# Four f32 projections of a decoder layer's chunk loop computed from high and low parts, with the loop's steps reordered on every engine

## The chip, the cores and the metric

The kernel runs on one core of a Trainium2 chip. The metric is the device time of one launch in microseconds (us). It was run three times, and the median is the time quoted.

## The reference

One decoder layer over x of shape (8, 512, 256): gated slot attention, cross-attention to 64 context rows per batch, and a top-2 mixture of eight experts. What matters here, cut:

```python
x = x + attn(layernorm(x))
    q, k = silu(x @ Wq), silu(x @ Wk);  v = x @ Wv
    f = log_sigmoid(x @ Wf) / 8;  s = 1 - exp(f)
    # recurrence over t: hk = hk*exp(f) + k s^T;  p = softmax(q hk);  hv = hv*exp(f) + s v^T;  o = p hv
    return rmsnorm(o) @ Wo
x = x + xattn(layernorm(x), ctx)      # softmax with distance bias; out @ W_o.T
x = x + ffn(layernorm(x))             # router, top 2 of 8, capacity 1280, W2(silu(W1 x) * W3 x)
```

## The kernel before, in words

The 4096 tokens are 32 chunks of 128. The first half of the program, the **chunk loop**, takes one chunk per step and is software-pipelined: each engine has a hand-written list in its own `step(run)`, and `run(lag, work)` does `work` for the chunk that is `lag` steps back. After 32 steps there are `LAGS` more, the **drain**. The second half, the **expert stage**, runs 40 groups of 256 rows and begins when the last routed row has been sent to memory by POOL (`send_rows`, indirect transfers).

The order of everything in the loop is set by these lists and by two kinds of semaphore wait: an operand's (`pe.wait_ge(f_cols_ok, n + 1)`), and a PSUM bank's, where `turns` lists which tiles share each of the eight banks and `bank_left` waits until the tile before has been read.

One chunk goes, in the program's names:

- DVE normalizes (`f_xn`, helper `norm`, L944), PE transposes it (`f_columns`, L1379), ACT copies it to SBUF as `f_xnt` (`evacuate`, L721).
- PE projects (`product`, L1385): `project_vf` for v and the gate (weights 128x512), `project_qk` for q, transposed (128x128), and k (128x256). Every operand is f32, and an f32 matmul runs as two passes: two records each.
- ACT: `f_absolute` (abs, exp, ln of the gate, L785 to L794), `qk_sigmoid` (three passes, L799 to L805), `one_minus`, `gates` (`down`, `decay`, `up`). DVE: `log_gates` (`g_s`, L1022), `queries_keys`, `slot_values` (`s_s`), then the state `hk`, `hv`. POOL adds two chunks' gates (`both_gates`, `g_both`, L603) and does the small powers of each norm.
- PE: `sum_states`, `sum_gates`, transposes, `scores`, `logits`; DVE, ACT and DVE do the softmax, PE transposes it (`p_columns`), ACT copies it (`p_t`), PE does `mix` and `read_out`, and `o_columns` / `project_o` give the block's output `y`, 128x256. The cross-attention follows with `x_scores`, `e_columns`, `values`, `x_outputs` (DVE, `xo_t`), `x_project_o` (`xy`, 128x256) and `residual2`; the router with `top_two` and `places` (DVE) and `send_rows` (POOL).

At the start, the first step also builds the context tables: `context_keys` (PE, and ACT's copies `k_all`, L776), `context_values`, and DVE's `small_tables`, which SP's `key_biases` waits for before it loads further rows of x. During the drain, `behind(c)` splits two of the six pieces of the first expert's weights after each of the drain's first three steps: the high half on ACT (L876), the low half on DVE (L1289, 128x1024 each).

The expert stage already multiplies split operands:

```python
def split_product(dst, pairs):
    return product(dst, [(lhs[i], rhs[k]) for lhs, rhs in pairs for i, k in ((0, 0), (0, 1), (1, 0))])
```

Its tiles are of type F32R, written as `hi = copy(t)` and `lo = t - hi`; each F32R matmul is one record.

## Time and profile before

| | us |
|---|---|
| runs | 1402.39, 1397.52, 1398.87; median 1398.87 |
| profiled execution, its own time | 1398.93 |
| its span, first to last instruction | 1397.2 |
| chunk loop, steady: from the normalization (`f_xn`) of chunk 3 to that of chunk 31 | 74.4 to 626.9, 19.73 a chunk |
| drain: from there to the last transfer that POOL issues | 626.9 to 702.0 |
| first matmul of the expert stage's tiles to the end | 707.4 to 1397.2 |
| busy: PE, DVE, ACT, POOL over the span | 93%, 67%, 46%, 30% |

The profile's busy shares are averages over stages with different limits. In the expert stage PE works almost without a gap; in the chunk loop PE and DVE are both close to full, ACT is a little over half busy. A row of a timeline gives start, duration, engine, line, operation, tiles and count, and in brackets how long the engine had been idle before it and what ended that. An instruction's result is visible a little after its duration ends, and the next independent instruction of the same engine can start before it ends.

### The profile page before, as it was taken

How to read it: one execution, taken by the hardware profiler on the slowest of the kernel's cores; microseconds unless marked ns; L12 is line 12 of the kernel's file. 1: busy time of each engine (PE TensorE's matmuls, PEld its weight loads, DVE VectorE, ACT ScalarE, POOL GpSimd, SP SyncE).
4: the chain of work that ended last, by engine and by line, in shares of the span. 5: the costliest groups of instructions: out<-in, count | busy, mean ns of one | idle time of the engine just before them, and what ended most of it. 6: DMA issues, size and time to landing. Idle time of an engine off the chain costs nothing.

```text
span 1397.2 us, 33423 instructions
## 1 busy us (share of the span) xinstructions
PE 1299.0 (93%) x11085; PEld 1153.5 (83%) x11085; DVE 931.1 (67%) x2770; ACT 640.2 (46%) x1628; POOL 417.4 (30%) x741
## 2 busy tenths in 40 slices
PE   7799999999999999998579999999999999999996
PEld 5577777777777777776369999999999999999996
DVE  5578888888888888887546565565645656565442
ACT  2355555555555555554344344443434435444331
POOL 4114334443444344433302122222221222211112
PEclk9899999999999999997579999999999999999999
DMA  3821210100101010100042242423524334252212
GB/s 96 248 86 34 96 54 25 34 30 30 33 26 34 26 34 25 34 23 24 27 132 31 32 121 32 122 33 48 116 33 113 37 64 94 34 123 32 31 24 24
DMA packets 152459, 80.20 MB, mean 57 GB/s; under 512 B 106210, under 2 KB 145859, under 8 KB 152290
## 3 DMA queue, kind: packets, MB, share of 16 engines
q1 hardware_dynamic: 137698, 59.11, 16.6%
q0 software_dynamic: 14592, 18.91, 7.9%
q8 instruction: 97, 1.59, 0.5%
q14 instruction: 72, 0.59, 0.1%
HBM read 44.04 MB, written 33.96 MB: 56 GB/s over the span
## 4 chain that ended last, share of the span: by engine, by line
PE 80%; DVE 7%; ACT 6%; issue 4%; DMA 1%; POOL 1%; SPq 0%; ACTq 0%; DVEq 0%; POOLq 0%
PE banks L1385 65%; PE banks L1494 4%; PE banks L1379 3%; PE banks L1569 2%; PE banks L1580 2%; PE banks L1489 2%; ACT qk_l L801 1%; ACT qk_e L799 1%; PE banks L1565 1%; DVE r_st L933 1%; DVE hk L1058 1%; DMA xin<-in_x 1%; ACT p_t L721 1%; ACT one_less L811 1%; DVE hv L1059 1%
## 5 line engine op out<-in xcount | busy, mean ns | idle before, releaser
L906 ACT ACTIVATE h_a<-banks 128x256 f32<-128x256 f32 x320 | 122.3, 382 | 348.1 <-PE banks L1385 333.1
L1316 DVE TENSOR_TENSOR h_f<-banks,h_a 128x256 f32<-128x256 f32 x320 | 135.6, 424 | 144.4 <-ACT h_a L906 119.7
L521 POOL TENSOR_TENSOR idle_g<-half 128x1 f32<-128x1 f32 x144 | 32.0, 222 | 533.4 <-DVE y_s L1335 383.0
L1385 PE MATMUL banks<-xe_t_hi,w_even_hi 128*128 128x256 f32 x640 | 180.6, 282 | 3.6 <-issue 2.1
L1385 PE MATMUL banks<-xe_t_hi,w_even_lo 128*128 128x256 f32 x640 | 180.4, 282 | 0.9 <-issue 0.9
L1385 PE MATMUL banks<-xe_t_lo,w_even_hi 128*128 128x256 f32 x640 | 180.4, 282 | 0.0
L1385 PE MATMUL banks<-xe_t_hi,w_odd_hi 128*128 128x256 f32 x640 | 178.2, 279 | 0.0
L1385 PE MATMUL banks<-xe_t_lo,w_odd_hi 128*128 128x256 f32 x640 | 178.2, 278 | 0.0
L1385 PE MATMUL banks<-xe_t_hi,w_odd_lo 128*128 128x256 f32 x640 | 178.2, 278 | 0.0
L895 ACT ACTIVATE h_t_hi<-h_f 128x256 fp32r<-128x256 f32 x320 | 131.7, 412 | 32.6 <-DVE h_f L1316 32.1
L1323 DVE TENSOR_TENSOR h_t_lo<-h_f,h_t_hi 128x256 fp32r<-128x256 f32 x320 | 133.6, 417 | 6.0 <-ACT h_t_hi L895 3.4
L700 POOL DMA_INDIRECT out_dram<-y_s,token x80 | 127.7, 1596 | 26.0 <-issue 19.2
L1385 PEld LDWEIGHTS banks<-xe_t_hi,w_even_hi 128*128 128x128 f32 x640 | 123.5, 193 | 4.2 <-issue 4.2
L1385 PEld LDWEIGHTS banks<-xe_t_hi,w_even_lo 128*128 128x128 f32 x640 | 122.4, 191 | 1.2 <-issue 1.2
L1385 PEld LDWEIGHTS banks<-xe_t_lo,w_even_hi 128*128 128x128 f32 x640 | 122.4, 191 | 0.0
L1385 PEld LDWEIGHTS banks<-xe_t_hi,w_odd_hi 128*128 128x128 f32 x640 | 121.4, 190 | 0.0
L1385 PEld LDWEIGHTS banks<-xe_t_lo,w_odd_hi 128*128 128x128 f32 x640 | 120.1, 188 | 0.0
L1385 PEld LDWEIGHTS banks<-xe_t_hi,w_odd_lo 128*128 128x128 f32 x640 | 120.1, 188 | 0.0
L1385 PE MATMUL banks<-w_in,f_xnt 128*128 128x512 f32 (+1 forms) x256 | 96.7, 500 | 0.5 <-ACT f_xnt L721 0.5
L1333 DVE CAST token<-about 128x1 uint32<-128x1 f32 x78 | 8.4, 149 | 127.0 <-PE banks L1385 127.0
L1385 PE MATMUL banks<-w_odd_hi,h_t_hi 128*128 128x256 f32 x320 | 89.1, 278 | 1.8 <-DVE h_t_lo L1323 1.8
L1385 PE MATMUL banks<-w_even_hi,h_t_hi 128*128 128x256 f32 x320 | 89.0, 278 | 0.0
(244 smaller groups left out, 3399.6 us busy)
## 6 DMA issues: line engine op xcount, KB each, us to landing
raw<-in_w SPq DMA_DIRECT2D x24, 1024.0 KB, 5.0
expert_rows<-empty SPq DMA_DIRECT2D x4, 2580.0 KB, 10.9
x_blocks<-expert_rows SPq DMA_DIRECT2D x312, 32.0 KB
xin<-in_x SPq DMA_DIRECT2D x32, 128.0 KB, 2.2
out_dram<-x SPq DMA_DIRECT2D x32, 128.0 KB, 1.7
out_dram<-y_s,token POOLq DMA_INDIRECT x80, 4.0
mask_i<-in_mask SPq DMA_DIRECT2D x32, 32.0 KB, 1.9
expert_rows<-r_xn,send POOLq DMA_INDIRECT x64, 2.6
```

The lines of the kernel that those rows point to most:

```text
L521: return pool.tensor_tensor(idle_g[:, i:i + 1], half[:, 0:1], half[:, 0:1], ALU.add)
L700: pool.indirect_dma_start(out=out, out_offset=bass.IndirectOffsetOnAxis(ap=token[par][a][:, :], axis=0), in_=y_s[:, par, a, :], in_offset= ...
L895: act.activation(h_t[0][:, par, f, :], h_f[:, f % 2, :], ACT.Copy).then_inc(h_hi_ok, 1)
L906: act.activation(h_a[:, f % 2, :], bank[2 + f % 4][:, 0:GS], ACT.Silu).then_inc(silu_ok, 1)
L1316: dve.tensor_tensor(h_f[:, f % 2, :], bank[2 + f % 4][:, GS:2 * GS], h_a[:, f % 2, :], ALU.mult)\
L1323: dve.tensor_tensor(h_t[1][:, par, f, :], h_f[:, f % 2, :], h_t[0][:, par, f, :], ALU.subtract)\
L1379: last = pe.transpose(dst[0:t.shape[1], i * P:(i + 1) * P], t, ident[:, :])
L1385: last = pe.matmul(dst, lhs, rhs, start=(i == 0), stop=(i == len(pairs) - 1))
L1489: pe.matmul(dst[:, m * P:(m + 1) * P], queries[:, m, :], states[:, m, :], start=True, stop=False)
L1494: last = pe.matmul(dst[:, cols], weights[:, h, :], rows[:, cols], start=False, stop=(h % 2 == 1))
L1569: last = pe.matmul(tile[f"x_scores{i}"][:, k * D:(k + 1) * D], xq_t[rows, k, :], k_bd[rows, k, :, :].rearrange("p h k -> p (h k)"), start= ...
L1580: last = pe.transpose(tile[f"e_cols{k}"][:, j * P:(j + 1) * P], pair, ident[:, :])
```

## The change

Four products of the chunk loop (v and gate, k, the attention's output, the cross-attention's output) take tiles of type F32R in a high and a low part, `hi*hi + hi*lo + lo*hi`, in place of one f32 product. The q projection stays f32. Chunk 0 still projects v, gate and k in f32.

```diff
+            def three(rows, weights, cols):
+                return [(rows[i][:, k, :], weights[j][:, k, cols]) for k in range(KT) for i, j in ((0, 0), (0, 1), (1, 0))]
...
             def project_vf(n, c, b):
-                pe.wait_ge(f_cols_ok, n + 1)
...
+                else:
+                    pe.wait_ge(f_lo_ok, n + 1)
+                    if n == 1:
+                        pe.wait_ge(weights_lo_ok, 1)
+                    pairs = three(f_part, w_in_part, slice(D, 3 * D))
                 bank_left(pe, "vf", n)
-                product(tile["vf"], [(f_xnt[:, k, :], w_in[:, k, 2 * D:4 * D]) for k in range(KT)]).then_inc(vf_mm, 1)
+                product(tile["vf"], pairs).then_inc(vf_mm, 1)
...
             def project_o(n, c, b):
-                pe.wait_ge(o_ok, n + 1)
+                pe.wait_ge(o_lo_ok, n + 1)
...
-                product(tile["y"][:, 0:D], [(o_t[:, k, :], wo_s[:, k, :]) for k in range(2)]).then_inc(y_mm, 1)
+                product(tile["y"][:, 0:D], three(o_part, wo_part, slice(0, D))).then_inc(y_mm, 1)
```

The parts are made by new instructions: ACT writes `f_hi` beside `f_xnt` and `xo_hi`, POOL writes `f_lo` and `xo_lo`, ACT's copy of the attention output becomes `o_hi` and DVE writes `o_lo`.

```diff
             def f_columns(n, c, b):
-                evacuate(n, f_xnt[:, :, :], two(tile["f_cols"][:, 0:D]), f_cols_mm, qk_mm, f_cols_ok)
+                if later(n, 1):
+                    act.wait_ge(qk_mm, n)
+                    act.wait_ge(f_lo_ok, n)
+                act.wait_ge(f_cols_mm, n + 1)
+                act.activation(f_xnt[:, :, :], two(tile["f_cols"][:, 0:D]), ACT.Copy)
+                act.activation(f_part[0][:, :, :], two(tile["f_cols"][:, 0:D]), ACT.Copy).then_inc(f_cols_ok, 1)
+                if not later(n, 1):
+                    act.wait_ge(vf_landed, 32)
+                    act.wait_ge(qk_landed, 32)
+                    act.activation(w_in_part[0][:, :, :], w_in[:, :, 0:3 * D], ACT.Copy).then_inc(weights_hi_ok, 1)
...
+            def f_low(n, c, b):
+                pool.wait_ge(f_cols_ok, n + 1)
+                if later(n, 1):
+                    pool.wait_ge(qk_mm, n)
+                pool.tensor_tensor(f_part[1][:, :, :], f_xnt[:, :, :], f_part[0][:, :, :], ALU.subtract).then_inc(f_lo_ok, 1)
+                if not later(n, 1):
+                    pool.wait_ge(weights_hi_ok, 1)
+                    pool.tensor_tensor(w_in_part[1][:, :, :], w_in[:, :, 0:3 * D], w_in_part[0][:, :, :], ALU.subtract)\
+                        .then_inc(weights_lo_ok, 1)
+            def xo_low(n, c, b):
...
+                pool.wait_ge(xo_hi_ok, n + 1)
+                pool.tensor_tensor(xo_part[1][:, :, :], xo_t[:, :, :], xo_part[0][:, :, :], ALU.subtract).then_inc(xo_lo_ok, 1)
...
+            def xo_high(n, c, b):
...
+                act.wait_ge(xot_ok, n + 1)
+                act.activation(xo_part[0][:, :, :], xo_t[:, :, :], ACT.Copy).then_inc(xo_hi_ok, 1)
...
+            def o_low(n, c, b):
+                dve.wait_ge(o_ok, n + 1)
+                dve.tensor_tensor(o_part[1][:, :, :], two(tile["o_cols"][:, 0:D]), o_part[0][:, :, :], ALU.subtract).then_inc(o_lo_ok, 1)
...
                 for k in range(KT):
                     dve.tensor_scalar(wo_s[:, k, :], wo_raw[:, k, :], gn[:, 0:1], None, ALU.mult).then_inc(small_made, 1)
+                dve.wait_ge(small_made, KT)
+                dve.tensor_copy(wo_part[0][:, :, :], wo_s[:, :, :]).then_inc(small_made, 1)
+                dve.wait_ge(small_made, KT + 1)
+                dve.tensor_tensor(wo_part[1][:, :, :], wo_s[:, :, :], wo_part[0][:, :, :], ALU.subtract).then_inc(small_made, 1)
```

To make room in SBUF, the third weight matrix of the even experts moves behind the chunk loop's tiles, so its two pieces of expert 0 are split in the first expert group and not in the drain:

```diff
             def behind(c):
-                if c < 3:
+                if c < 2:
                     for piece in (2 * c, 2 * c + 1):
                         split_weights(0, 0, piece)
...
+                    if is_last(g, 0) and f in (1, 2):
+                        split_weights(0, 0, 3 + f)
```

The four lists are reordered, and their beginnings moved round (`LAGS` is 6 for that reason; a lag that is one higher at a list's start is the same place in the program as one lower at its end). POOL's new list is `both_gates, r_power, values, x_power, keys, f_power_later, hidden_keys, send_rows, f_low, xo_low, head_power`. PE, from the transposes of `f_xn` (`sum_states` adds k and v to the states; `before` and `all_b` are the router's counts); before:

```order
L1379 MATMUL banks<-ident,f_xn 128x128 x2
...
L1385 MATMUL banks<-w_in,f_xnt 128x512 x2
L1385 MATMUL banks<-f_xnt,w_in 128x128 x4
L1385 MATMUL banks<-w_in,f_xnt 128x256 x2
L1385 MATMUL banks<-both,before 128x8
L1385 MATMUL banks<-both,all_b 128x8
L1385 MATMUL banks<-s_s,k_s 64x64 x4
L1385 MATMUL banks<-v_s,s_s 64x64 x4
L1385 MATMUL banks<-g_s,tri_half 128x256
```

and in the change:

```order
L1446 MATMUL banks<-ident,f_xn 128x128 x2
...
L1452 MATMUL banks<-s_s,k_s 64x64 x4
L1452 MATMUL banks<-v_s,s_s 64x64 x4
L1452 MATMUL banks<-w_in_hi,f_hi 128x512
L1452 MATMUL banks<-w_in_lo,f_hi 128x512
L1452 MATMUL banks<-w_in_hi,f_lo 128x512
...
L1452 MATMUL banks<-f_xnt,w_q 128x128 x4
L1452 MATMUL banks<-w_in_hi,f_hi 128x256
...
L1452 MATMUL banks<-both,before 128x8
```

`sum_states` now stands between `read_out` (left out in both) and `project_vf`. DVE, from the end of `places` to the router's statistics (`zk`, `zv` are `end_states`, `x` is `residual2`); before:

```order
L1230 TENSOR_TENSOR send<-slot_f,off_f 128x2
L1068 TENSOR_TENSOR zk<-banks,hk 128x256
L1069 TENSOR_TENSOR zv<-banks,hv 128x256
L1031 TENSOR_TENSOR q_t<-banks,qk_s 128x256
L1032 TENSOR_TENSOR k_s<-banks,qk_s 128x256
L1041 SCALAR_TENSOR_TENSOR s_s<-one_less,down 128x256
L1166 TENSOR_TENSOR x<-banks,x 128x256
L933 BN_STATS r_st<-x 128x6
```

and in the change:

```order
L1294 TENSOR_TENSOR send<-slot_f,off_f 128x2
L1230 TENSOR_TENSOR x<-banks,x 128x256
L1090 TENSOR_TENSOR q_t<-banks,qk_s 128x256
L1091 TENSOR_TENSOR k_s<-banks,qk_s 128x256
L1193 TENSOR_TENSOR o_lo<-banks,o_hi 128x256
L1100 SCALAR_TENSOR_TENSOR s_s<-one_less,down 128x256
L988 BN_STATS r_st<-x 128x6
```

`zk` and `zv` have moved up to stand behind `b_ms` (`head_squares`), ahead of `sc` (`x_less`); `x` has moved ahead of `q_t`, and `o_lo` is new. ACT at the very start of the change, where before `f_abs` follows `f_xnt` at once and `k_all` comes after `s_t`:

```order
L764 ACTIVATE f_xnt<-banks 128x256
L765 ACTIVATE f_hi<-banks 128x256
L769 ACTIVATE w_in_hi<-w_in 128x1536
L818 ACTIVATE k_all<-banks 128x512 x2
L827 ACTIVATE f_abs<-banks 128x256
```

The two `k_all` copies of the context keys have moved ahead of the gate's `f_abs`.

## Rows read from the trace of the kernel before

**Rows 1.** The page, part 1: busy us (share of the span) and instructions, two engines.

```profile
PE 1299.0 (93%) x11085; PEld 1153.5 (83%) x11085; DVE 931.1 (67%) x2770; ACT 640.2 (46%) x1628; POOL 417.4 (30%) x741
```

**Rows 2.** Windows: length, busy us (count) of PE, PEld, DVE, ACT, POOL, clock, DMA.

```profile
200.00:300.00 100.00, 93.84 (x844) 72.91 (x842) 83.89 (x287) 54.72 (x141) 41.30 (x83) 1.00 0.09 30
660.00:700.00 40.00, 22.36 (x141) 15.43 (x140) 20.60 (x80) 12.35 (x25) 15.23 (x38) 0.59 0.09 30
800.00:1400.00 600.00, 581.29 (x4999) 580.40 (x4997) 327.11 (x795) 242.22 (x617) 129.47 (x144) 0.99 0.34 63
```

**Rows 3.** The chain of waits, one period of the loop: start, us, what.

```profile
291.62 0.39 ACT p_t L721
...
296.03 3.54 PE banks L1385 x16
...
299.60 0.61 ACT qk_e L799
...
311.50 0.39 ACT p_t L721
```

**Rows 4.** Timeline of PE in that period.

```profile
295.87 1.94 PE L1385 MATMUL banks<-w_in,f_xnt 128*128 128x512 f32 x4
...
299.40 0.17 PE L1385 MATMUL banks<-both,before 128*128 128x8 bf16 x1
...
299.52 0.45 PE L1385 MATMUL banks<-s_s,k_s 128*64 128x64 f32 x8
...
300.13 0.70 PE L1385 MATMUL banks<-g_s,tri_half 128*128 128x256 f32 x2
```

**Rows 5.** Timeline of ACT in that period.

```profile
295.16 0.38 ACT L721 ACTIVATE f_xnt<-banks 128x256 f32<-128x256 f32 x1 [2.43 <-PE banks L1379]
```

**Rows 6.** Timeline of POOL in that period.

```profile
299.85 0.73 POOL L603 TENSOR_TENSOR g_both<-g_s 128x256 f32<-128x256 f32 x1 [1.55 <-DVE g_s L1022]
```

**Rows 7.** Timeline of DVE in that period.

```profile
296.94 0.16 DVE L1121 SCALAR_TENSOR_TENSOR b_ms<-b_ss,b_floor 128x4 f32<-128x4 f32 x1
...
299.28 0.42 DVE L1022 SCALAR_TENSOR_TENSOR g_s<-banks,f_l 128x256 f32<-128x256 f32 x1 [0.52 <-ACT f_l L794]
299.64 0.17 DVE L1216 TENSOR_TENSOR place<-banks,taken 128x8 f32<-128x8 f32 x1
...
299.92 0.69 DVE L1219 TENSOR_TENSOR place_h<-hot,place 128x16 f32<-128x16 f32 x1
...
301.19 0.42 DVE L1068 TENSOR_TENSOR zk<-banks,hk 128x256 f32<-128x256 f32 x1
...
302.86 0.42 DVE L1166 TENSOR_TENSOR x<-banks,x 128x256 f32<-128x256 f32 x1
303.31 0.43 DVE L933 BATCH_NORM_STATS2 r_st<-x 128x6 f32<-128x256 f32 x1
```

**Rows 8.** Timeline of DVE, two periods earlier, where POOL adds no gates.

```profile
260.50 0.17 DVE L1219 TENSOR_TENSOR place_h<-hot,place 128x16 f32<-128x16 f32 x1
```

**Rows 9.** Timeline of PE at the start, after the context keys.

```profile
15.98 1.89 PE L1385 MATMUL banks<-xw,raw 128*128 128x256 f32 x8
```

**Rows 10.** Timeline of ACT at the start.

```profile
10.47 0.38 ACT L785 ACTIVATE f_abs<-banks 128x256 f32<-128x256 f32 x1 [3.87 <-PE banks L1385]
...
14.58 0.40 ACT L811 ACTIVATE one_less<-g_s 128x256 f32<-128x256 f32 x1
18.77 0.38 ACT L820 ACTIVATE down<-banks 128x256 f32<-128x256 f32 x1 [3.79 <-PE banks L1385]
...
20.98 1.09 ACT L776 ACTIVATE k_all<-banks 128x512 f32<-128x512 f32 x2
```

**Rows 11.** Timeline of DVE at the start, the wait for chunk 2's rows.

```profile
49.15 0.43 DVE L933 BATCH_NORM_STATS2 f_st<-xin 128x6 f32<-128x256 f32 x1 [5.24 <-DMA xin<-in_x]
```

**Rows 12.** Timeline of DVE in the drain, its second and third step.

```profile
671.46 0.17 DVE L1190 TENSOR_SCALAR r_lg<-banks 128x8 f32<-128x8 f32 x1 [4.82 <-PE banks L1385]
...
687.97 2.35 DVE L1289 TENSOR_TENSOR w_even_lo<-raw,w_even_hi 128x1024 fp32r<-128x1024 f32 x2
```

More of the change, by code:

```diff
@@ L117, in decoder_layer @@
         raw = [raw_of[m] for m in range(3)]
-        w_even = [[sb(f"w{m}_even_{part}", [P, 2, 4 * D], F32R) for part in ("hi", "lo")] for m in range(3)]
+        before_weights = ExitStack()
+        w_in = before_weights.enter_context(nc.sbuf_tensor("w_in", [P, KT, 3 * D], F32))
+        before_weights.close()
+        w_even = [[sb(f"w{m}_even_{part}", [P, 2, 4 * D], F32R) for part in ("hi", "lo")] for m in range(2)]
         tiles1 = ExitStack()
@@ L214, in decoder_layer @@
         w_odd = [[sb(f"w{m}_odd_{part}", [P, 2, 4 * D], F32R) for part in ("hi", "lo")] for m in range(3)]
+        w_even.append([sb(f"w2_even_{part}", [P, 2, 4 * D], F32R) for part in ("hi", "lo")])
         w_s = [w_even, w_odd]
@@ L672, in step @@
             def step(run):
+                run(1, both_gates)
                 run(4, r_power)
@@ L1258, in step @@
             def step(run):
+                run(2, sum_and_values)
+                run(1, f_norm_and_context)
+                run(2, mix_and_tables)
+                run(5, top_two)
                 run(3, x_maximum)
                 run(2, head_squares)
+                run(2, end_states)
                 run(3, x_less)
@@ L1433, in project_qk @@
                     product(tile["qk"][:, m * P:(m + 1) * P],
-                            [(w_in[:, k, m * P:(m + 1) * P], f_xnt[:, k, :]) for k in range(KT)])
-                product(tile["qk"][:, D:2 * D], [(f_xnt[:, k, :], w_in[:, k, D:2 * D]) for k in range(KT)])\
-                    .then_inc(qk_mm, 1)
+                            [(w_q[:, k, m * P:(m + 1) * P], f_xnt[:, k, :]) for k in range(KT)])
+                product(tile["qk"][:, D:2 * D], three(f_part, w_in_part, slice(0, D)) if later(n, 1) else
+                        [(f_xnt[:, k, :], w_in[:, k, 0:D]) for k in range(KT)]).then_inc(qk_mm, 1)
             def sum_gates(n, c, b):
@@ L1594, in x_project_o @@
             def x_project_o(n, c, b):
-                pe.wait_ge(xot_ok, n + 1)
+                pe.wait_ge(xo_lo_ok, n + 1)
+                if not later(n, 1):
+                    pe.wait_ge(weights_lo_ok, 2)
                 bank_left(pe, "xy", n)
-                product(tile["xy"][:, 0:D], [(xo_t[:, k, :], xw[:, 3, k, :]) for k in range(KT)]).then_inc(xy_mm, 1)
+                product(tile["xy"][:, 0:D], three(xo_part, xwo_part, slice(0, D))).then_inc(xy_mm, 1)
             def r_columns(n, c, b):
@@ L1651, in step @@
                 run(1, read_and_positions)
+                run(1, sum_states)
                 run(0, project_vf)
@@ L1665, in step @@
                 run(1, x_columns)
+                run(2, values)
+                run(3, r_columns)
+                run(1, x_queries)
+                run(0, p_columns)
+                run(3, r_logits)
             over_chunks(step)
```

136 lines of the change are left out of this document (74 added, 62 removed).

## The prediction, made before the change was run

> **What bounds the kernel now.** I read the page first: PE is busy for 93% of the span [rows 1], which says little, since two stages are averaged. The windows separate them: in the expert stage PE works 581 of 600 us, 0.116 us per F32R matmul of 256 columns; in the chunk loop it works 93.8 of 100 us while DVE works 83.9 [rows 2]. The change touches only the loop, so I then read the chain of waits there: one period runs from one `p_t` to the next, 291.62 to 311.50, 19.88 us [rows 3]. Of it the 16 records of the projections take 3.54 us; the rest passes through PE, ACT and DVE in turn. The timelines of one period show where DVE stops waiting: `g_s` at 299.28 is the last one that it is idle for (0.52 us, for ACT's `f_l`); `place` follows at 299.64 and then everything up to the softmax stands in one row without a gap [rows 7]. So the period is: the softmax, PE from `mix` to the end of the v and gate projection, ACT's four passes to `f_l`, and DVE's own queue from `g_s` on. A PE saving counts only if it lets `g_s` start earlier, and a DVE instruction after `g_s` counts in full.
>
> **The change, part by part: the loop.** The projections take 3.53 us (295.87 to 299.40) for 4096 columns in passes [rows 4], 0.86 ns a column; v and gate are 2048 of them, 1.77 us, k 1024, 0.88 us. As three F32R products, v and gate are six matmuls of 512 columns. At the expert stage's 0.116 us for 256 columns [rows 2] they cost at most 6 x 0.232 = 1.39 us; less the few ns of each start, I take 1.30. k, `y` and `xy` are six of 256 columns, 0.70 us, for 0.88. PE's work falls by 0.47 + 3 x 0.18 = 1.0 us a chunk, 32 us in all. Almost none of this reaches the period, for this reason:
>
> - `sum_states`, 0.61 us (299.52 to 300.13) [rows 4], now stands before the v and gate projection, which therefore cannot start before 295.87 + 0.61 = 296.48.
> - The projection also waits for `f_lo`. `f_xnt` starts at 295.16 and lasts 0.38 [rows 5]. From `zk` to `x` DVE takes 1.67 us for five passes of 0.42 [rows 7], 0.33 each, so a queued pass begins some 0.08 before the last ends; with the same on ACT, `f_hi` ends 0.30 after `f_xnt`, at 295.84. POOL has not shown this operation; its nearest row is the 128x256 addition `g_both`, 0.73 us [rows 6], also from two SBUF tiles. With 0.1 for each hand-over `f_lo` is there at 296.77, 0.29 us after `sum_states`. Bounds: 0.45 us for the subtraction (DVE's pace for this shape) and 1.1 (half as much again as `g_both`).
> - So v and gate end at 296.77 + 1.30 = 298.07, against 297.64: 0.43 us **later**, and `f_l`, `g_s` and `place` with them. The counts, which `place` also needs, now end at 298.07 + 0.88 (q) + 0.70 (k) + 0.2 = 299.85, before `place` at 300.07; they do not bind.
> - On DVE, from `place` to `r_st` it was 3.67 us [rows 7]. Now `zk` and `zv` (0.67) are gone from there, into the wait before `g_s`; `o_lo` comes in at 0.33; and `x` stands well ahead of `r_st`, which no longer waits for it (0.45 becomes 0.33). The stretch is 1.55 to the end of `send`, plus five steps of 0.33: 3.20 us, 0.47 **less**.
>
> Net, 0.43 - 0.47: -0.04 us a chunk at these hand-overs; with 0.05 for the two, which a few rows allow, -0.14. I take -0.08, times the 28 chunks between the third and the last: **-2.2 us**. The other additions are covered: `xo_hi` and the move of `top_two` by DVE's and ACT's waits before `b_ms`, `o_hi` ahead of `down` by DVE, which reaches `s_s` later than ACT does. `xo_lo` on POOL delays `b_w` to about 297.4, and `b_o` comes after `sc`, 1.2 us behind that. If that cover goes, each costs its 0.3 to 0.7 us a chunk.
>
> One row speaks of more. `place_h`, 16 elements a partition, takes 0.69 us where POOL adds the gates, and 0.17 in a chunk where it does not [rows 7, 8]; it ends when `g_both` ends [rows 6]. The two new POOL subtractions could hold DVE in the same way: `xo_lo` runs to about 297.4, and `b_ms`, due at 296.94, has two SBUF operands too. Then `zk`, `zv`, `sc` and `b_o` follow it, 2.2 us, and `g_s` could not start before 299.7. By the sum it starts at 299.71, so I count nothing; uncovered it would be 0.46 us a chunk, 13 us. The Trainium skill (SBUF — State Buffer, SBUF: two separate sides) states the rule: DVE instructions with two SBUF inputs and POOL's instructions hold one port pair in turn, each for its whole length. The trace agrees, 0.69 against 0.17 us; by that rule alone the sum would stay as it is, since the hold falls in a wait.
>
> **The start.** ACT now copies `k_all` before `f_abs`. `k_all` needs the context keys, which end on PE at 15.98 [rows 9], and takes 1.09, so `f_abs` moves from 10.47 to 17.1 [rows 10]. From `f_abs` to the end of `one_less` was 4.5 us [rows 10], part of it a wait for q and k that will be over by then; the passes themselves, five of 256 columns at some 0.35 and three of 512 at 0.61 [rows 3] and a little more, are 3.6. So `down` comes at 20.7, where it stood at 18.77, waiting for PE: +1.9 us. DVE's `small_tables` gets two passes of 512 elements, 1.1 us, by twice the 0.33 of 256 (0.67) for the subtraction and less for the copy. SP issues the load of chunk 2's rows after these tables, and DVE waits 5.24 us for that load [rows 11], so both shifts arrive in full: **+3.0 us** (bounds 1 and 4.5). The split of the input weights, 1536 elements on ACT and POOL, lies in the time before chunk 1 and costs nothing, unless POOL holds `s_s`; then 0.5.
>
> **The drain.** Three pairs of weight splits stand in it, 2.35 us of DVE each [rows 12]. The third leaves for the first expert group, where DVE is half idle [rows 2]: -2.3, but the last chunk's `xy` now waits for `xo_hi` and `xo_lo` (0.38 + 0.73 + 0.2) and gets 0.5 back on a slow PE, so -1.5. The second now stands before `top_two` and so falls into a wait of 4.82 us for the router's logits [rows 12] in place of following it: -2.3. The first moves ACT's halves ahead of `k_t` of the last chunk: +0.3. Together **-3.5 us** (bounds -7 and +1).
>
> **The sum.** 1398.93 (its own time) - 2.2 + 3.0 - 3.5 = 1396.2; the profiled execution stands at the median of the runs, 1398.87, so nothing is added. **Forecast: 1396**, 0.2% faster. What this kernel's measurement can tell from no change is about 0.3%, 4.2 us. Adding the bounds of the parts that are not rivals, 1390 to 1402.
>
> **The rivals.**
>
> - **The projection does not wait.** If `f_lo` is there by 296.48, the period falls by 0.29 more. For it: `f_xnt` starts 0.4 us after the transposes are drawn as ended, which may shift with the order. Against: `g_both`'s 0.73. 28 x 0.29 = 8: 1388.
> - **POOL becomes a link of the chain and costs more than it frees** (the slower side). Place: `f_lo` before `project_vf`, with `xo_lo` before `b_ms` behind it. Each 0.1 us that `f_lo` is later costs 2.8 us; the change turns slower when it takes over 0.83 us, and slower than the measurement can overlook from 0.98. At 1.0 us: 28 x 0.27 = 7.6, plus some 2 from the held `b_ms`: 1406. For it: POOL stands between two engines here for the first time in a period that has no slack, behind two indirect transfers. Against: those end a microsecond before `f_hi`.
> - **The clock falls in the loop.** PE loses 1 us of 17.8 of work a chunk and waits more. In the drain, where PE worked 22.4 of 40 us, the mean granted clock was 0.59, between the levels 1.2 and 2.4 GHz; in the loop it was 1.00 [rows 2]. A tenth of the loop at 1.2 GHz, 55 us, would add a share of 55 x 0.85 x 0.5 or so: 1415. Against: nothing in the loop comes near the drain's idle share. The Trainium skill (TensorE: Matmul & The Clock Gate, HAM oscillation) warns of kernels that idle between bursts of matmuls; the drain agrees, 0.59, and the loop does not show it.
> - **The products are no cheaper.** If an F32R pass of 512 columns cost as much as an f32 one, 0.44, v and gate would take 2.65: +0.9 a chunk, 1420. Against it stands the expert stage's 0.116.
>
> **How the numbers follow.** The sum as worked out 0.53, POOL not in the way 0.25, POOL as a link 0.15, the clock 0.03, dearer products 0.04. Of the first, a spread of 5 us puts 0.17 below 1394.7 and 0.05 above 1403.1. Faster: 0.17 + 0.25 = 0.42 less a little of the second, 0.41. Slower: 0.05 + 0.15 + 0.07 less a little, 0.25. The same: 0.34. The range takes in the first two and most of the third: 1384 to 1407.
>
> **What would show it.** In the loop: F32R matmuls of 512 columns 0.215 to 0.23 us apart; PE idle for some 0.3 us before them, ended by POOL's `f_lo`; `g_s` still followed by an unbroken row of DVE work; periods of 19.6 to 19.7 us, where they were 19.73 on average. At the start, chunk 2's wait ends near 52. In the drain, the stretch from the last `f_xn` to the last issue 71 to 72 us, where it was 75. Wrong would be: `f_lo` longer than 0.83; `b_ms` late and `g_s` released by nothing but DVE's queue; a clock below 1.00 between 100 and 600.

## The result: 0.4% slower, where 0.2% faster was forecast

The kernel before takes 1398.92 us (median of eight runs, 1397.52 to 1402.39), the changed one 1403.61 (eight runs, 1402.3 to 1410.55). The ratio is 1.0038, 95% interval 1.0023 to 1.0054. The time lies within the forecast range, but the change goes the other way than forecast. The profiled execution took 1403.64 us, its span 1401.6, against 1398.93 and 1397.2 before. From the timelines of both I took five points and the stretches between them, in us (the last `f_xn` is that of chunk 31):

| stretch | before | after | difference | forecast |
|---|---|---|---|---|
| start, to `f_xn` of chunk 3 | 74.44 | 82.61 | +8.2 | +3.0 |
| loop, 28 periods | 552.45 | 556.92 | +4.5 | -2.2 |
| drain, last `f_xn` to last issue of `expert_rows` | 75.11 | 68.77 | -6.3 | -3.5 |
| from there to the first expert product | 8.01 | 8.13 | +0.1 | 0 |
| expert stage | 687.19 | 685.17 | -2.0 | 0 |

The last row is not the change's: in the profiles of the experiments below the same expert stage takes 683 to 689 us. What is left is two losses larger than forecast and a gain larger than forecast.

**The profile after.** The page's busy line, which answers to [rows 1], and windows (length, busy us and count of PE, PEld, DVE, ACT, POOL, then clock, DMA share, GB/s), which answer to [rows 2] with two for the start:

```profile
PE 1283.5 (92%) x11337; PEld 1168.6 (83%) x11337; DVE 939.3 (67%) x2804; ACT 657.2 (47%) x1694; POOL 473.1 (34%) x807
```

```profile
0.00:35.00 35.00, 24.60 (x99) 16.98 (x99) 14.17 (x41) 10.10 (x21) 17.45 (x59) 0.90 0.30 93
35.00:60.00 25.00, 17.11 (x99) 13.98 (x100) 15.04 (x53) 7.40 (x20) 5.58 (x9) 0.70 0.68 191
...
200.00:300.00 100.00, 90.76 (x869) 74.78 (x868) 84.56 (x289) 56.74 (x151) 49.16 (x95) 1.00 0.10 30
...
660.00:700.00 40.00, 24.99 (x195) 19.21 (x195) 26.42 (x92) 11.96 (x27) 18.19 (x31) 0.70 0.09 31
800.00:1400.00 600.00, 586.19 (x5054) 585.59 (x5053) 331.41 (x806) 245.92 (x627) 134.68 (x146) 0.99 0.35 64
```

PE has 3 us less work in 100 us of the loop and the loop is not shorter, which is what the prediction said of PE's savings. The clock in the loop is 1.00. The same period of the loop as in rows 3 to 7 follows, ten microseconds later (it begins with the product of chunk 14, the third of its sequence): the timelines of PE, ACT, POOL and DVE.

```profile
305.27 0.45 PE L1452 MATMUL banks<-s_s,k_s 128*64 128x64 f32 x8
...
305.88 0.50 PE L1452 MATMUL banks<-w_in_hi,f_hi 128*128 128x512 f32 x1
306.22 0.39 PE L1452 MATMUL banks<-w_in_lo,f_hi 128*128 128x512 f32 x1
306.45 0.40 PE L1452 MATMUL banks<-w_in_hi,f_lo 128*128 128x512 f32 x1
...
307.38 1.05 PE L1452 MATMUL banks<-f_xnt,w_q 128*128 128x128 f32 x8
...
312.28 0.44 PE L1446 MATMUL banks<-ident,decay 128*128 128x128 f32 x2 [1.20 <-ACT decay L873]
```

```profile
304.17 0.38 ACT L764 ACTIVATE f_xnt<-banks 128x256 f32<-128x256 f32 x1 [2.62 <-PE banks L1446]
304.45 0.38 ACT L765 ACTIVATE f_hi<-banks 128x256 fp32r<-128x256 f32 x1
```

```profile
304.91 0.72 POOL L621 TENSOR_TENSOR f_lo<-f_xnt,f_hi 128x256 fp32r<-128x256 f32 x1 [0.82 <-ACT f_hi L765]
305.60 0.73 POOL L635 TENSOR_TENSOR xo_lo<-xo_t,xo_hi 128x256 fp32r<-128x256 f32 x1
```

```profile
306.25 0.16 DVE L1180 SCALAR_TENSOR_TENSOR b_ms<-b_ss,b_floor 128x4 f32<-128x4 f32 x1
...
309.02 0.42 DVE L1081 SCALAR_TENSOR_TENSOR g_s<-banks,f_l 128x256 f32<-128x256 f32 x1 [0.47 <-ACT f_l L836]
309.36 0.16 DVE L1280 TENSOR_TENSOR place<-banks,taken 128x8 f32<-128x8 f32 x1
...
309.64 0.72 DVE L1283 TENSOR_TENSOR place_h<-hot,place 128x16 f32<-128x16 f32 x1
...
311.94 0.42 DVE L1193 TENSOR_TENSOR o_lo<-banks,o_hi 128x256 fp32r<-128x256 f32 x1
...
312.61 0.42 DVE L988 BATCH_NORM_STATS2 r_st<-x 128x6 f32<-128x256 f32 x1
```

Three things are to be seen. `f_lo` takes 0.72 us and is there at 305.63, within `sum_states` (to 305.88), so PE does not wait for it. The six v and gate products take 1.50 us (305.88 to 307.38), the first 0.34 and the others 0.23 each. And `place` to `r_st` is 3.25 us, where it was 3.67 [rows 7]. PE's new wait of 1.20 us for `decay` comes in every chunk; whether it costs anything, the experiments say.

**The loop in three segments.** The prediction's period was a cycle: v/gate product to `g_s` (PE, ACT), `g_s` to `b_p` (DVE without a gap, then the softmax), `b_p` to the next v/gate product (PE). From the timelines of PE and DVE I took each segment for all chunks and averaged over the seven of a kind: chunk 0 of a sequence has no state before it and no `g_both`; in chunk 1 POOL builds `k_bd`.

| chunk of the sequence | before: to `g_s` / to `b_p` / to v/gate | sum | after | sum | difference |
|---|---|---|---|---|---|
| 0 | 3.42 / 10.43 / 5.30 | 19.16 | 3.14 / 10.25 / 6.04 | 19.43 | +0.27 |
| 1 | 3.42 / 11.26 / 5.29 | 19.97 | 3.15 / 11.05 / 6.05 | 20.25 | +0.28 |
| 2 | 3.41 / 11.25 / 5.28 | 19.95 | 3.14 / 10.84 / 6.02 | 20.00 | +0.05 |
| 3 | 3.42 / 11.15 / 5.28 | 19.85 | 3.15 / 10.72 / 6.06 | 19.93 | +0.08 |

The first and third segment change alike in all chunks, -0.28 and +0.75, together +0.47. The second gives back 0.42 in chunks 2 and 3, but 0.2 in chunks 0 and 1. The loop's loss is mostly in these two. Single chunks stand 0.2 to 0.36 above their kind in both kernels (chunk 18 by 0.36 after, chunk 12 by 0.35 before). With medians in place of means the second segment gives back 0.11, 0.16, 0.44 and 0.45 in chunks 0 to 3: the same finding.

In chunk 0, DVE does not fill the time that it has gained. In chunk 16, the first of its sequence, it reaches `q_t` early and waits for ACT:

```profile
350.93 0.42 DVE L1090 TENSOR_TENSOR q_t<-banks,qk_s 128x256 f32<-128x256 f32 x1 [0.32 <-ACT qk_s L847]
```

**The start.** ACT, then PE at the start of the changed kernel, and DVE's wait for chunk 2's rows ([rows 9 to 11] before):

```profile
16.01 1.09 ACT L818 ACTIVATE k_all<-banks 128x512 f32<-128x512 f32 x2 [7.00 <-PE banks L1452]
16.98 0.39 ACT L827 ACTIVATE f_abs<-banks 128x256 f32<-128x256 f32 x1
```

```profile
18.90 0.70 PE L1452 MATMUL banks<-g_s,tri_half 128*128 128x256 f32 x2 [1.20 <-DVE g_s L1081]
...
21.10 0.69 PE L1446 MATMUL banks<-ident,decay 128*128 128x128 f32 x2 [1.07 <-ACT decay L873]
...
23.12 1.22 PE L1452 MATMUL banks<-q_t,k_t 64*128 64x128 f32 x8 [0.47 <-ACT k_t L802]
```

```profile
55.84 0.43 DVE L988 BATCH_NORM_STATS2 f_st<-xin 128x6 f32<-128x256 f32 x1 [5.30 <-DMA xin<-in_x]
...
56.59 0.41 DVE L999 TENSOR_SCALAR x_xn<-x,x_mv,x_rstd 128x256 f32<-128x256 f32 x1
```

`f_abs` and the shift of DVE's tables came as worked out (16.98 for 17.1; `wo_hi` and `wo_lo` 1.1). Two things are new. PE waits 1.20 and 1.07 us for the late gates, and then it runs at 1.2 GHz for some 6 us: the granted clock is 0.50 from 22 to 26 us and 1.00 again from 28, and the eight `q_t,k_t` matmuls take 1.22 us, where they took 0.71. And `x_xn` of chunk 0 now stands behind `f_statistics`, which waits 5.30 us for a DMA; before, it ran ahead of that wait.

### The profile page after: what moved, and what is told of

Read it like the earlier page. It is cut to its first block, busy times and chain, and to the rows that moved or that the text cites. A ratio compares the mean times of both kernels' runs of the same rounds, so it can differ in the third digit from the quotient of the medians.

```text
span 1401.6 us, 34185 instructions
## 1 busy us (share of the span) xinstructions
PE 1283.5 (92%) x11337; PEld 1168.6 (83%) x11337; DVE 939.3 (67%) x2804; ACT 657.2 (47%) x1694; POOL 473.1 (34%) x807
## 4 chain that ended last, share of the span: by engine, by line
PE 80%; DVE 7%; ACT 6%; issue 4%; DMA 1%; POOL 1%; SPq 0%; ACTq 0%; DVEq 0%; POOLq 0%
PE banks L1452 66%; PE banks L1446 4%; PE banks L1570 3%; PE banks L1645 2%; PE banks L1565 2%; PE banks L1656 2%; ACT qk_l L843 1%; ACT qk_e L841 1%; PE banks L1641 1%; DMA xin<-in_x 1%; DVE hk L1117 1%; ACT o_hi L754 1%; DVE hv L1118 1%; ACT down L872 1%; DVE o_lo L1193 1%
## 5 line engine op out<-in xcount | busy, mean ns | idle before, releaser
L1452 PE MATMUL banks<-w_even_hi,h_t_lo 128*128 128x256 f32 x320 | 88.8, 278 | 0.0
```

What stands on the lines that cost most here:

```text
L1452: last = pe.matmul(dst, lhs, rhs, start=(i == 0), stop=(i == len(pairs) - 1))
```

## The experiments

All are compared with the kernel before on the same chip. Here "start" is `f_xn` of chunk 3, "period" the mean of the 28 after it, and "phase" that mean for one kind of chunk, from its `f_xn` to the next; all three are from one profiled execution of each kernel. The experiments ran on several chips, so between two of them the ratios compare and the microseconds only roughly. Starts scatter: `third_pair` and the kernel before are the same program up to the drain, and their `f_xn` of chunk 3 are at 73.54 and 74.44; another such pair differs by 1.6 us at chunk 1 (below).

**Order and products apart.** `order_only` puts the four products back to f32 and drops all parts; `products_only` keeps the parts and puts the four lists back, with the new steps at these places (the weights' third pair stays in the first expert group in both):

```diff
 # products_only: before's lists, LAGS = 5, before's bank turns, and
+                run(0, f_low)       # POOL, behind hidden_keys
+                run(3, xo_low)
+                run(4, xo_high)     # ACT, behind f_columns
+                run(2, o_low)       # DVE, behind queries_keys
```

> The changed kernel with all four products in f32 again and without the parts of tiles and weights: the new order alone (and two weight pairs in the drain). Theory (the order loses the time at the start and a little per chunk): f_xn of chunk 3 starts at 79 to 82 us (74.44 before, 82.61 changed), the period in the loop stays at 19.8 to 20.0 us, the time is 1400 to 1405. Rival (the split work on ACT, POOL and DVE loses it): f_xn of chunk 3 by 76, period 19.6 to 19.7, time 1390 to 1396.

> The changed kernel with its four engines in the order of before: the split products alone (and two weight pairs in the drain). Theory (order loses at the start; products need an order that hides f_lo): f_xn of chunk 3 at 75 to 77 us, but the v/gate product waits for f_lo behind ACT 0.38 + POOL 0.72 in each chunk, less the 0.47 it is shorter: period 20.1 to 20.4, time 1402 to 1415. Rival (the products cost at the start and nothing later): f_xn of chunk 3 at 79 to 82, period 19.5 to 19.7, time 1396 to 1400.

`order_only`: 1412.58 us, ratio 1.0117 (1.0102 to 1.0131); start 77.92, period 20.22. `products_only`: 1467.76 us, 1.0525 (1.0501 to 1.0548); start 77.30, period 21.96. Neither forecast held, in start, period or time. The order alone costs 0.49 us a chunk, far more than I thought; the products in the old order cost 2.2. Together they cost 0.16: **in the new order the products are worth 0.33 us a chunk**. The segments of `order_only` say which: 3.46 to `g_s`, where the changed kernel has 3.14, and 6.02 to v/gate, as in the changed kernel. So the 0.75 that the third segment lost is the order's, not a wait for `f_lo`. In `products_only` such waits are there: PE for `f_lo` 21.0 us in 23 chunks, DVE's `o_lo` for ACT's `o_hi` 12.6. That is partly the places I chose, so its 2.2 is no price of the products as such.

At the start, the two PE lines of `order_only` that answer to those above:

```profile
20.36 0.44 PE L1424 MATMUL banks<-ident,decay 128*128 128x128 f32 x2 [1.07 <-ACT decay L857]
...
21.94 0.71 PE L1430 MATMUL banks<-q_t,k_t 64*128 64x128 f32 x8 [0.65 <-DVE hv L1091]
```

The same waits, 0.74 us earlier, and the clock stayed at 2.4 GHz: `f_xn` of chunk 1 is at 30.08 instead of 33.46. So the order alone starts 3.5 us late, and the other 4.7 are seen only in the changed kernel. Of these 3.4 are there by chunk 1: 0.74 from before `decay`, the other 2.6 under the lower clock. The next experiment shows that this lower clock is not a fixed price of the products. `products_only` starts 2.9 us late with both moves undone and the clock at 1.00 between 20 and 36 us; that is 1.8 more than the 1.1 us of `wo`'s parts, and no run shows where.

**The two moves at the start.**

```diff
 # keys_act: ACT
                 run(3, x_columns)
+                run(2, context_keys)
...
-                run(1, context_keys)
 # x_first: DVE
                 run(1, scores_and_context)
-                run(0, f_statistics)
                 run(2, x_norm)
+                run(0, f_statistics)
```

> The changed kernel with ACT's context_keys (k_all) back in its place behind x_columns. Theory (k_all ahead of f_abs delays the first gates, and the clock falls with it): f_xn of chunk 1 back by 3 to 4 us from 33.46, chunk 3 by 3 to 5 us from 82.61, time 1399 to 1401. Rival (what follows waits for chunk 2's load of x anyway): chunk 1 back, chunk 3 by less than 1 us, time 1403 to 1404. The loop's period stays 19.89 in both.

> The changed kernel with DVE's x_norm ahead of f_statistics, as before. Theory (behind f_statistics the x chain of chunk 1 waits for the load of chunk 2, 5.3 us, and then stands in the way on PE and ACT): f_xn of chunk 3 back by 1 to 3 us from 82.61; in the loop x_norm waits 0.7 us for POOL's rstd ahead of f_statistics, 0 to 0.3 us per chunk more, time 1401 to 1410. Rival (the order of these two matters for the loop alone, since chunk 2's load lands when it does): f_xn of chunk 3 within 0.5 us of 82.61, time 1403 to 1412.

`keys_act`: 1400.41 us, 1.0021 (1.0009 to 1.0034); start 79.82, period 19.88. `f_xn` of chunk 1 is 3.5 us earlier and that of chunk 3 2.8, a little less than the 3 expected. This restores ACT's order, and the clock of chunk 0 is 1.00. In time the gain is not clear: the interval meets the changed kernel's (1.0023 to 1.0054). `x_first`: 1412.54 us, 1.0107 (1.0092 to 1.0122); start 80.18, 2.4 us earlier, period 20.22, 0.33 longer. But 1.6 of these 2.4 us are there at `f_xn` of chunk 1, at 31.88 instead of 33.46, and the move first acts behind that point: up to there the two programs are the same. The difference is one between executions. PE met the same two waits 1.07 us later than in the changed kernel's profile (`decay` at 22.17 us, behind a wait of 1.07) and kept its clock, 1.00 from 16 to 40 us; the eight `q_t,k_t` matmuls at 23.74 take 0.71 us. So `x_first` gives the move 0.9 us at the start (`f_xn` of chunk 1 to that of chunk 3, 48.30 for 49.15), and the better measurement is `x_first_start` below. In the loop `x_norm` belongs behind, where `f_statistics` covers POOL's `x_rstd`. That wait is 0.18 us in 23 chunks of `x_first`; the rest of the 0.33 was not traced. (The chunk whose `x_norm` stands behind the load is chunk 0; the expectations call it chunk 1.)

**What stands in DVE's stretch.** From here on each kernel is built on `keys_act`. `y_f32` puts y's product back to f32, without `o_lo` and `wo`'s parts; `f_split_only` does the same with xy, without `xo_hi` and `xo_lo`.

```diff
 # y_f32
-                product(tile["y"][:, 0:D], three(o_part, wo_part, slice(0, D))).then_inc(y_mm, 1)
+                product(tile["y"][:, 0:D], [(o_t[:, k, :], wo_s[:, k, :]) for k in range(KT)]).then_inc(y_mm, 1)
...
-                run(2, o_low)
```

> keys_act with y's product in f32 again, without o_lo on DVE and without the parts of wo at the start. Theory (a cycle sets the loop: b_p, PE to v/gate, ACT to g_s, then DVE without a gap to b_p; o_lo stands in that DVE stretch for 0.33 us, while the longer f32 product falls into PE's waits of 1.20 and 0.61 us): period 19.876 less 0.2 to 0.33 = 19.55 to 19.68, chunk 3's f_xn 1 us earlier from wo's parts, time 1389 to 1394. Rival (PE's busy time sets the loop): PE grows by 0.25 us per chunk, period 20.0 to 20.15, time 1403 to 1408.

> y_f32 with x's output product in f32 too, without xo_hi on ACT and xo_lo on POOL: of the split products v/gate and k alone are left. Theory (xo's parts stand outside the cycle, its product between k and the gates has 1.20 us of PE's wait behind it): period within 0.1 us of y_f32, time within 2 us of it, 0 to 2 us less at the start. Rival (gates wait behind the longer product, POOL's two lows delay b_w): period 0.1 to 0.3 us away from y_f32 in either direction.

`y_f32`: 1394.08 us, 0.9970 (0.9958 to 0.9981), period 19.74, start 80.40. `f_split_only`: 1395.03 us, 0.9968 (0.9948 to 0.9987), period 19.74. **The split of y is a loss**: PE's f32 product is longer and the kernel is faster, since DVE is the limit there and PE waits. The gain is 0.14 a chunk, less than 0.2 to 0.33: the segment to `b_p` falls by 0.21 to 0.25 in chunks 1 to 3, and rises by 0.15 in chunk 0. That is 3.8 us in the loop; the rest of the gain in time lies in the drain and the expert stage and is not explained. The split of xy is worth nothing either way. From `order_only`'s 20.22 to 19.74, the splits of v, gate and k alone are worth 0.47 a chunk. The start did not gain its microsecond.

**POOL's `k_bd`.** It now stands between `x_rstd` and `f_rstd`. `k_bd_back` puts it behind `send_rows` again.

```diff
-                run(2, keys)
                 run(0, f_power_later)
                 run(1, hidden_keys)
                 run(5, send_rows)
+                run(1, keys)
```

> keys_act with POOL's keys (k_bd) back behind send_rows. Theory (k_bd between x_rstd and f_rstd holds DVE once in four chunks; the period of that chunk is 20.21): that period falls to 19.9 to 20.0, mean 19.80 to 19.83, time 1398 to 1399. Rival (k_bd then delays f_lo, which is on the cycle, in that chunk): that period 20.3 to 21.3, time 1401 to 1408.

1407.76 us, 1.0072 (1.0058 to 1.0086); the other three phases are unchanged, the one in question went from 20.21 to 21.37. The direction is the rival's, but its cause was not, as DVE's and POOL's timelines of this kernel show:

```profile
442.39 2.92 DVE L1267 TENSOR_TENSOR hot<-expert_no,top_f 128x16 f32<-128x16 f32 x1
445.34 0.17 DVE L1273 TENSOR_TENSOR both<-hot 128x8 bf16<-128x8 f32 x1
```

```profile
442.69 1.21 POOL L648 TENSOR_TENSOR k_bd<-k_all,diag 128x256 f32<-128x256 f32 x2
443.83 0.75 POOL L621 TENSOR_TENSOR f_lo<-f_xnt,f_hi 128x256 fp32r<-128x256 f32 x1
444.52 0.74 POOL L635 TENSOR_TENSOR xo_lo<-xo_t,xo_hi 128x256 fp32r<-128x256 f32 x1
```

`hot`, 16 elements a partition and 0.17 us elsewhere, takes 2.9 us, from 0.3 us before `k_bd`'s row begins, while that of POOL's indirect transfer is still open, until the last of four POOL instructions in a row (`k_bd` is two) has ended. This is so in five of the loop's seven chunks of this kind; in a sixth `both` takes 2.70 in its place, and in the first `hot` and `both` take 0.63 and 1.21. PE did not wait for `f_lo`; it waited 1.51 us ahead of the counts, whose bank DVE's `b_o` leaves at 449.3, late for the same reason. The same hold, smaller, is what `k_bd` costs in its new place. The changed kernel with `k_bd` (POOL, then DVE), and DVE one chunk later without it; `x_xn` takes 0.70 us in six of the seven such chunks:

```profile
455.50 1.18 POOL L648 TENSOR_TENSOR k_bd<-k_all,diag 128x256 f32<-128x256 f32 x2
```

```profile
456.13 0.70 DVE L999 TENSOR_SCALAR x_xn<-x,x_mv,x_rstd 128x256 f32<-128x256 f32 x1
...
476.30 0.41 DVE L999 TENSOR_SCALAR x_xn<-x,x_mv,x_rstd 128x256 f32<-128x256 f32 x1
```

The Trainium skill (SBUF — State Buffer, SBUF: two separate sides) says that the one engine holds the port pair for its whole instruction. The trace agrees for `k_bd`, 0.70 against 0.41; it goes further in `k_bd_back`, where DVE did not get its turn between POOL's instructions either.

**The start once more.** `x_first_start` is `y_f32` with `x_norm` ahead of `f_statistics` for chunks 0 and 1 only. `x_first_start_load` adds an earlier load of chunk 2's rows, and `before_load` is that edit in the kernel before:

```diff
             for c in range(2 * CPB):
-                step(c // CPB, c % CPB)
+                if c != 1:
+                    step(c // CPB, c % CPB)
                 if c == 0:
+                    step(0, 1)
                     key_biases()
```

> y_f32 with x_norm ahead of f_statistics for chunks 0 and 1 alone. Theory (at the start the x chain of chunk 1 stands behind the wait for chunk 2's load, 5.55 us, and then in the way of p_cols and of the next chunk; in the loop f_statistics belongs first): chunk 3's f_xn 2 to 5 us earlier than 80.40, period 19.74 as in y_f32, time 1389 to 1392. Rival (that loss is a clock of 1.2 GHz in the wait's wake, whatever the order): chunk 3's f_xn within 1 us of 80.40, time 1393 to 1395.

> x_first_start with SP's load of x for chunk 2 (and its mask) issued right behind chunk 1's, ahead of its waits for the tables of key and query positions. Theory (DVE waits 5.2 to 5.6 us for this load, and PE falls to 1.2 GHz behind it): chunk 3's f_xn 6 to 10 us earlier than in x_first_start, time 1380 to 1385. Rival (the tables' own path, key_biases and query_places for the first x_scores, ends at the same point): 0 to 3 us earlier.

> The kernel before with the same early load. Theory: chunk 3's f_xn from 74.44 to 66 to 70 us, time 1389 to 1394. Rival (tables' path): 1397 to 1399.

`x_first_start`: 1392.61 us, 0.9958 (0.9943 to 0.9973), start 76.94. `x_first_start_load`: 1386.39, 0.9910 (0.9893 to 0.9927), start 71.10. `before_load`: 1391.20, 0.9953 (0.9936 to 0.9970), start 67.72. The order of `x_norm` and `f_statistics` moves the start by 3.5 us, with `f_xn` of chunk 1 in its place (29.92 and 30.10), as expected; in time this is not clear of noise. The early load moves it by 5.8, just short of the 6 expected, and by 6.7 in the kernel before. The times are 0.6 and 1.4 us above the expected ranges for the first two and inside for the third. `start_only` is the changed kernel with all its splits and these three moves:

> The changed kernel with the three moves at the start alone (k_all behind x_columns, x_norm ahead of f_statistics for chunks 0 and 1, the early load of chunk 2), all four split products kept. Theory (start and loop add up): chunk 3's f_xn at 70.5 to 73 us, period 19.88, time 4 to 6 us above x_first_start_load = 1390 to 1392. Rival (the parts of wo at the start delay the first y and the tables once more): chunk 3's f_xn at 74 or later, time above 1393.

1392.02 us, 0.9946 (0.9932 to 0.9959), start 69.28, 1.2 us earlier than the range expected, period 19.88. Against `before_load` 1.6 us are left of the start's loss, with all the splits in place, hardly more than starts scatter. Most of the loss goes with the moves.

**The drain.** `third_pair` is the kernel before with its third pair of weight splits in the first expert group.

> The kernel before with the third pair of weight splits taken out of the drain and put into the first group of the expert stage: that step of the change alone. Theory (it stands on DVE's path for 2.35 us in the drain and the first group has room): 1395.5 to 1397.5, last issue of expert_rows 71.5 to 73.5 us behind the last f_xn (75.1 before). Rival (the drain waits elsewhere, or the first group pays it back): 1397.5 to 1401.

1398.37 us, 1.0007 (0.9994 to 1.0020). The stretch from the last `f_xn` to the last issue is 73.56, 1.55 less, as forecast for this step (-1.5); in the total it can't be told from nothing, and `before_load`, which leaves the drain as it is, has 74.27, 0.8 less too. The rest of the drain's 6.3 is the order's, since `order_only` has the same 68.77. Its size is rough: `keys_act` and `x_first`, which have the changed kernel's drain but for one move each, take 70.23 and 71.43.

**The chunk without a state.** On top of `x_first_start_load`, ACT's `o_columns` goes back behind `gates` (`down`, `decay`, `up`), and then POOL's `keys` into its idle stretch behind `head_power`.

```diff
 # down_first: ACT
                 run(1, one_minus)
-                run(2, o_columns)
                 run(1, gates)
+                run(2, o_columns)
 # down_first_keys: POOL, too
-                run(2, keys)
...
                 run(1, head_power)
+                run(1, keys)
```

> x_first_start_load with ACT's o_columns behind gates (down, decay, up) again. Theory (in the chunk without a state before it DVE is not the limit but ACT's chain from qk_e over one_less and o_t to down, 0.27 us of it o_t): the period of that phase from 19.52 to 19.25 to 19.35, the other phases within 0.05 of 19.68, 20.02 and 19.78, time 1.5 to 2.5 us less. Rival (o_t then comes late for y's product, which stands ahead of the scores on PE): all phases 0.1 to 0.3 longer.

> down_first with POOL's keys (k_bd) behind head_power of the same pass. Theory (k_bd, 1.19 us for two, between x_rstd and f_rstd holds f_rstd back and DVE's x_xn; behind b_w POOL is idle for 2 us): the period of that phase from 20.02 to 19.7 to 19.85, time 1 to 2 us less than down_first. Rival (there it delays g_both, and with it the gates, or holds DVE at b_o and g_s): 20.0 to 20.4.

`down_first`: 1381.93 us, 0.9877 (0.9861 to 0.9893). Chunk 0's phase fell from 19.52 to 19.24 as expected, and the other phases by 0.11 to 0.13, which was not. `down_first_keys`: **1377.92 us, 0.9851 (0.9834 to 0.9868), 1.5% faster than before**; the phase with `k_bd` fell from 19.89 to 19.65, the others stayed within 0.02. From one of these kernels to the next the intervals of the ratio meet or overlap, so what each step does is read from the phases. Its timelines of POOL and DVE show the hold gone:

```profile
425.22 1.18 POOL L649 TENSOR_TENSOR k_bd<-k_all,diag 128x256 f32<-128x256 f32 x2
```

```profile
434.41 0.41 DVE L1000 TENSOR_SCALAR x_xn<-x,x_mv,x_rstd 128x256 f32<-128x256 f32 x1
```

**`sum_states` ahead of v/gate.** Is this the step that loses? Three kernels, the first on `keys_act`, the others on `down_first_keys`:

```diff
 # states_back: PE and DVE
-                run(1, sum_states)   # PE, ahead of project_vf
...
                 run(4, counts)
+                run(1, sum_states)
...
-                run(2, end_states)   # DVE, ahead of x_less
                 run(5, places)
+                run(2, end_states)
 # states_residual_back: DVE, too
-                run(4, residual2)    # ahead of queries_keys
                 run(1, slot_values)
+                run(4, residual2)
 # pe_tail_back: PE, too, behind sum_states
-                run(1, o_columns)
-                run(3, x_project_o)
                 run(0, sum_gates)
+                run(3, x_project_o)
+                run(1, o_columns)
```

> keys_act with PE's sum_states back behind the counts and DVE's end_states back behind places. Theory (the v/gate product starts when f_lo is there, 0.1 to 0.3 us earlier; zk and zv, 0.68 us, stand in DVE's stretch from g_s to b_p again): period 19.876 plus 0.4 to 0.6 = 20.25 to 20.5, time 1411 to 1418. Rival (sum_states ahead of v/gate is pure loss of 0.61 on PE's path, zk and zv fall into DVE's waits): period 19.3 to 19.8, time 1385 to 1398.

> down_first_keys with sum_states behind the counts (PE), end_states behind places and residual2 behind slot_values (DVE) as before. Theory (sum_states costs the path from b_p to v/gate 0.61 us, less what v/gate would wait for f_lo, about 0.4, so 0.2; zk and zv out of DVE's stretch behind g_s give back 0.68; the move is a gain of 0.3 to 0.5): period 19.53 to 19.85 to 20.05, time 1386 to 1393. Rival (on the path the move is a loss of 0.61 and PE would not wait for f_lo): 19.0 to 19.5, time 1364 to 1377.

> states_residual_back with PE's sum_gates, x_project_o and o_columns in this order behind sum_states, as before, so that DVE reads the sums before o_columns needs their bank. Theory (zk and zv in DVE's stretch behind g_s cost 0.68, v/gate starts 0.2 earlier): no wait of 1.98 on PE, the clock stays at 2.4 GHz, period 19.85 to 20.05, time 1386 to 1393. Rival (without the bank's wait the old place is the better one): 19.0 to 19.5, time 1364 to 1377.

The first two gave 1489.06 us, 1.0656 (1.0642 to 1.0671), and 1479.63, 1.0591 (1.0569 to 1.0614), periods 22.77 and 22.90: much worse than either theory, so they answer another question. PE's timeline of `states_residual_back`:

```profile
421.31 0.61 PE L1451 MATMUL banks<-ident,b_o 128*128 128x128 f32 x2 [1.98 <-issue]
421.57 0.56 PE L1457 MATMUL banks<-xwo_hi,xo_hi 128*128 128x256 f32 x1
...
422.36 0.41 PE L1457 MATMUL banks<-xwo_hi,xo_hi 128*128 128x256 f32 x1
```

`o_columns` writes the bank of the sums and waits 1.98 us until DVE has read them (`zv`, 420.79 to 421.20). Behind that wait the clock is at 1.2 GHz (0.41 us for a matmul that takes 0.28 at 2.4), and between 100 and 600 us it is 0.91 to 0.97 on average in stretches of 100 us. `pe_tail_back`, where the bank is free in time: 1394.44 us, 0.9965 (0.9952 to 0.9978), period 19.93, as the theory said, the time 1.4 us above it. To v/gate 5.81 instead of 6.02 (PE now waits 0.35 for `f_lo`), to `b_p` 0.16 more in chunk 0 and 0.7 to 0.8 more in the others. **The moves together (`sum_states`, `end_states`, `residual2` and PE's tail) are a gain of 0.39 us a chunk**, for all that they cost PE's segment; `sum_states` alone was not tried. This does not contradict `order_only`, where the whole new order loses 0.49: there is no `f_lo` to wait for there, so the third segment pays 0.74 for the order, where here it pays 0.2.

## Why the prediction was wrong, by its own steps

- **The bound of the loop**: right. The cycle of the prediction is the one that sets the period; `y_f32` (PE longer, kernel faster) and `pe_tail_back` show it. The new PE wait of 1.20 us costs nothing there.
- **v and gate 0.43 us later, and `g_s` with them**: right in the sum, +0.47, wrong in its parts. The product takes 1.50, not 1.30, and saves 0.27: the expert stage's 0.116 for 256 columns carries over to the pace, 0.23 for 512, but each group's first matmul takes 0.34. k takes 0.79 for the 0.70 expected and 0.87 before, so PE's work falls by some 0.5 us a chunk, not by 1.0. `f_lo`, 0.72 for the 0.73 taken, is no wait at all. Instead the segment `b_p` to v/gate has 0.14 more than `sum_states`' 0.61, in `order_only` too. On PE 0.10 of it lie between the last matmuls of `read_out` and what follows them: 0.49 us to `sum_states`, where it was 0.39 to v/gate. Why is open.
- **0.47 less on DVE from `place` to `r_st`, times 28 chunks**: this is the step that failed in the loop. The loop was to gain 0.08 us a chunk and lost 0.16; of these 0.24, 0.16 lie here, since DVE's stretch gave 0.31 on average. In chunks 2 and 3 it gave 0.42. In chunk 1 half is lost to `k_bd`, beside which `x_xn` takes 0.29 longer, and `down_first_keys` gets 0.24 of it back. I had named this hold, but looked for it at `b_ms`, where it did not come (0.16), and overlooked `keys` in POOL's new list. In chunk 0 `place_h` is not held (0.17) and `hk` and `hv` are only cleared, so DVE waits for others: in chunk 16 `place` to `r_st` is 3.10 for 3.37, with 0.32 of waiting for `qk_s`, and 0.14 more behind `hv`, before the residual of the attention output. Taking `zk` and `zv` out of its way saves little, while `sum_states` costs its 0.61 in full. One ordinary period was read and multiplied by 28; the trace had all four kinds. `o_hi` ahead of `down`, put down as covered by DVE, was not covered in the kernels without `o_lo`: `down_first` gave 0.28 in chunk 0 and 0.11 to 0.13 in the others. With `o_lo` ahead of `s_s`, as in the changed kernel, this was not tried.
- **The 0.05 for the two hand-overs**, of which I had taken about half: not there.
- **The start, +3.0 with bounds 1 and 4.5**: the second failed step, +8.2. Its two terms came about as worked out (`decay` 1.6 us later, for `down`'s 1.9, and 1.1). Missing were 2.4 us between `decay` and `f_xn` of chunk 1, the price of PE's lower clock in this execution, and 3.1 us more from there to chunk 3. Part of the 3.1 is the order of `x_norm` and `f_statistics`, which I had read as a move in the loop alone: 0.9 in `x_first`, 3.5 in `x_first_start`, which is another kernel. How much of the 8.2 another execution of the changed kernel would show is open: `x_first` ran the same program up to chunk 1 without the lower clock.
- **The drain, "-3.5"**: the direction right, -6.3, inside the bounds of -7 and +1. The third pair gave -1.55 for -1.5; the rest was undersized. The mean clock over the drain is 0.77 where it was 0.70, which I had not counted (the page's window of 660 to 700 us, 0.70 for 0.59, cuts a different part of the drain in each kernel). How the rest divides between clock and waits was not tried.
- **The rivals.** The projection does not wait: its condition came true, its gain did not, since `sum_states` stands there anyway. POOL as a link: `f_lo` was below its point of 0.83, yet POOL is in the way by what it holds. The clock falls in the loop: not in this kernel, 1.00; it did at the start, in one execution, and `states_back` shows the case, period 22.8 and a clock of 0.88 to 0.97 in stretches of 100 us. The Trainium skill's warning (TensorE: Matmul & The Clock Gate, HAM oscillation), that PE loses its clock again and again where it idles between bursts of matmuls, fits that kernel and `states_residual_back`. Dearer products: no, they are worth 0.33 a chunk.

The sum of the errors in the two failed steps, 5.2 at the start and 6.7 in the loop, less 2.8 in the drain and 2.0 of the expert stage's scatter, gives 7.1 of the 7.4 us between the forecast of 1396.2 and the profiled execution's 1403.64. That the time lies inside the range owes to the range's width and to the drain, not to the mechanism.

## What to carry to other kernels

Where a loop has kinds of iterations, take the cycle's segments for each kind before multiplying: an engine that has slack in one kind turns a saving there into nothing, while the cost stays. A reordering has to be read once more for the first iterations, in which a step may stand behind a DMA it never waits for later, and a new wait of a microsecond on PE can, in some executions, cost more through the clock than by itself. A difference at the start between two profiles is the edit's only from the first instruction on that the edit can reach. Undo such a change along the banks and queues it is tied to, or the experiment measures a stall of its own.

## What the runs showed of the hardware that was not expected

- POOL's instructions in a row can hold a DVE instruction with two SBUF operands through all of them: 2.92 us for one of 0.17, in five of seven chunks of `k_bd_back`.
- A product in three F32R matmuls a tile pays 0.34 us for its first matmul of 512 columns and 0.23 for each other; 0.20 and 0.12 for 256 columns (`k`, 308.19 to 308.98).
- The granted clock after the same two waits of PE, 1.20 and 1.07 us, was 1.2 GHz in the changed kernel's profile and 2.4 in two others: in `order_only`, with these waits 0.74 us earlier, and in `x_first`, with the same program up to there and the waits 1.07 us later. Which it will be could not be read from the waits.
